# Output and base projections of a transformer block on eight cores: the block loop taken in interleaved pairs

## The chip, the cores and the metric

The kernel runs on the 8 NeuronCores of one Trainium2 chip. All cores run the same program on different rows of the input. The metric is the device time in microseconds (us) of the slowest core; lower is better.

## The reference

```python
x = L0_attn_hidden_states                    # (4, 2048, 2048) float32
xn = _layernorm(x)                           # no scale, no bias
# attention: q, k, v = xn @ Wq.T, xn @ Wk.T, xn @ Wv.T; 16 heads of 128
probs = softmax(q @ k.T * HEAD_DIM ** -0.5)
attn  = (probs @ v) @ Wo.T
# second branch: a base projection and one of 8 rank-16 experts per token
base_out = xn @ W_base.T + b_base
onehot   = one_hot(argmax(softmax(xn @ router_W.T)), 8)
h        = einsum('bsd,erd->bser', xn, A) * onehot[..., None]
delta    = einsum('bser,eor->bso', h, Bw)
return x + attn + base_out + delta * 2.0
```

## The kernel before

Each core owns 1024 tokens of one of the four sequences (QOWN) and computes keys and values for all 2048 tokens of it, so that no core talks to another. Everything is kept transposed: features on the 128 partitions, tokens along the free dimension, matmul operands in bf16, sums in PSUM in float32.

The work has four stages. The first (ln_stats, ln_norm, router, mask_chain) normalizes the tokens and writes xnT, 16 chunks of 128 features by 2048 tokens, which stays on the chip. The second (b2) computes hm, the masked expert activations. The third goes over the 16 heads: the projections of head h are woven into the scores of head h-1, and the result of every head goes into ctall (16 chunks of 128 features by 1024 tokens).

The fourth stage is the one that the change touches. It makes the output in 16 blocks oc of 128 output features by 1024 tokens. A block has two parts:

- gen_dpre(oc), a generator that emits one step at a time. It issues the block's loads: Wo's slice into wot (line 518) and W_base's slice into wbv (line 521) on POOL's queue, both cast from float32 to bf16 on the way, and the residual xT (line 525) on SP's queue. Then it emits 32 matmuls W_base x xnT (line 531: 16 feature chunks, two halves of 512 tokens) and 2 matmuls of the expert weights wbls x hm (line 539), one matmul in each step.
- dpost(oc) emits 32 matmuls Wo x ctall (line 554) onto the same PSUM sums, then one VectorE instruction (line 560) that adds bias and residual and writes outb, and the store outT<-outb on SP's queue (line 565).

Even blocks use PSUM tile psB, weights wqs (Wo) and wks (W_base), and the first half of xst and outb; odd blocks use the upper half of psA, wvs (Wo) and vt (W_base), and the second half. These are the buffers of the attention stage, used again, so every block has two buffers of each kind to alternate with and no third.

Every instruction is recorded by emit() in the order of the Python code, and each engine executes its own instructions in that order. emit() gives an instruction the waits that its buffers need: the last writer of what it reads, the last writer and the readers of what it overwrites. A load of wqs for block oc+2 thus waits for the last matmul of dpost(oc). DMA-issuing instructions stand in the queue of POOL or SP in the order of emission, and one that waits holds all behind it in its queue.

Blocks 0 and 1 are different: gen_dpre(0) and gen_dpre(1) are woven into the scores of the last head, and dpost(0) and dpost(1) follow each other once that head is finished. From block 2 on, gen_dpre(oc) and dpost(oc) alternate.

Of the kernel before, what the change touches and what calls it, by code (L numbers as in the profile page):

```python
# [16 lines left out]
NDC = 16  # L17
# [130 lines left out]
def build_program(debug=False):  # L148
# [28 lines left out]
    with ExitStack() as st:  # L177
# [62 lines left out]
        def xnt(dc, lo, hi):  # L240
            return xnT[:, dc * SEQ + lo: dc * SEQ + hi]
# [262 lines left out]
        def dpsum(oc):  # L504
            if oc % 2 == 0:
                return psB, 0, ["psB0", "psB1"]
            return psA, 1024, ["psA2", "psA3"]

        def gen_dpre(oc):
            ps_t, off, pk = dpsum(oc)  # L510
            if oc % 2 == 0:
                wot, wok_keys = wqs, ["wqs"]
                wbv, wbk_keys = wks[:, 0:D], ["wks"]
            else:
                wot, wok_keys = wvs, ["wvs"]
                wbv, wbk_keys = vt[:, 0:D], ["vt0", "vt1"]
            dstate[oc] = (wot, wok_keys)
            p.emit("pool", lambda E, oc=oc, wot=wot: E.dma_start(
                wot[:, 0:D], wo4[oc].rearrange("p a b -> p (a b)")),
                writes=wok_keys)  # L520
            p.emit("pool", lambda E, oc=oc, wbv=wbv: E.dma_start(
                wbv, wb4[oc].rearrange("p a b -> p (a b)")), writes=wbk_keys)
            sl = oc % 2
            xv = xst[:, sl * D: sl * D + QOWN]
            p.emit("sync", lambda E, oc=oc, xv=xv: E.dma_start(
                xv, xT[oc * 128:(oc + 1) * 128, :]), writes=[f"xs{sl}"])
            yield
            for dc in range(NDC):
                for nb in range(2):
                    p.emit("pe", lambda E, dc=dc, nb=nb, ps_t=ps_t, off=off,  # L530
                           wbv=wbv, wbk_keys=wbk_keys, pk=pk: E.matmul(  # L531
                        ps_t[:, off + nb * 512: off + (nb + 1) * 512],
                        wbv[:, dc * 128:(dc + 1) * 128],
                        xnt(dc, nb * 512, (nb + 1) * 512),
                        start=(dc == 0), stop=False),
                        reads=wbk_keys + XNALL, writes=[pk[nb]])
                    yield
            for nb in range(2):
                p.emit("pe", lambda E, oc=oc, nb=nb, ps_t=ps_t, off=off, pk=pk: E.matmul(
                    ps_t[:, off + nb * 512: off + (nb + 1) * 512],  # L540
                    wbls[:, oc * 128:(oc + 1) * 128],
                    hm[:, nb * 512:(nb + 1) * 512],
                    start=False, stop=False),
                    reads=["wbls", "hm"], writes=[pk[nb]])
                yield

        def dpost(oc):
            ps_t, off, pk = dpsum(oc)
            wot, wok_keys = dstate[oc]
            sl = oc % 2  # L550
            xv = xst[:, sl * D: sl * D + QOWN]
            for dc in range(NDC):
                for nb in range(2):
                    p.emit("pe", lambda E, dc=dc, nb=nb, ps_t=ps_t, off=off, wot=wot: E.matmul(  # L554
                        ps_t[:, off + nb * 512: off + (nb + 1) * 512],
                        wot[:, dc * 128:(dc + 1) * 128],
                        ctall[:, dc * QOWN + nb * 512: dc * QOWN + (nb + 1) * 512],
                        start=False, stop=(dc == NDC - 1)),
                        reads=wok_keys + ["ct"], writes=[pk[nb]])
            p.emit("dve", lambda E, oc=oc, sl=sl, xv=xv, ps_t=ps_t, off=off, pk=pk: E.scalar_tensor_tensor(  # L560
                outb[:, sl * QOWN:(sl + 1) * QOWN],
                ps_t[:, off: off + 1024],
                bbs[:, oc:oc + 1], xv, ALU.add, ALU.add),
                reads=pk + ["bbs", f"xs{sl}"], writes=[f"outb{sl}"])
            p.emit("sync", lambda E, oc=oc, sl=sl: E.dma_start(
                outT[oc * 128:(oc + 1) * 128, :],
                outb[:, sl * QOWN:(sl + 1) * QOWN]),
                reads=[f"outb{sl}"], writes=[], dsem=f"d_out{sl}")
# [28 lines left out]
        attn_av(NH - 1, 1)  # L597
        dpost(0)
        dpost(1)
        for oc in range(2, NDC):  # L600
            for _ in gen_dpre(oc):
                pass
            dpost(oc)

        if debug:
            for name, src, reads in [
# [21 lines left out]
def _get_nc(debug=False):  # L628
    if debug not in _NC_CACHE:
        _NC_CACHE[debug] = build_program(debug)  # L630
    return _NC_CACHE[debug]
# [59 lines left out]
```

How the kernel before makes its waits and increments, by code:

```python
            def body(E, items=items, eng=eng):  # L133
                for it in items:
                    if it[0] == "w":
                        E.wait_ge(sem[it[1]], waitval(it[1], it[2]))
                    else:
                        instr = it[1](E)
                        sname = it[2]
                        if (sname, it[3]) in tgt:
                            instr.then_inc(
                                sem[sname],
                                16 if sname in self.dma_sems else 1)
```

## Time and profile before

| | us |
|---|---|
| median of 2 runs | 1283.63 (1283.35 to 1283.91) |
| the profiled execution, its own time | 1283.7 |
| its span, from the first to the last instruction, slowest core (6) | 1282.2 |
| the spans of the eight cores | 1275.3 to 1282.2 |
| TensorE busy in it | 1142.7 (89%) |

The profile is of one execution on the slowest core. Times inside it count from the start of the span. "PE" is TensorE's matmuls, "PEld" its weight loads, "DVE" VectorE, "SPq" and "POOLq" are the queues on which SP and POOL issue DMAs. PEclk or clock is the share of the full TensorE clock that was granted. L531 means line 531 of the kernel. Tile names leave out buffer numbers, so "psA" is any of psA's banks. Ends of matmuls are modelled: a single one shows 379 ns, though one starts every 216 ns.

### The profile page before, as it was taken

To read this page: it belongs to the slowest core of one execution; us is meant where nothing else is said; L and a number is where in the kernel's file an instruction comes from. 1 tells how busy PE (TensorE), PEld (TensorE's weight loads), DVE (VectorE), ACT (ScalarE), POOL (GpSimd) and SP (SyncE) were. 2 spreads that over 40 slices of the span, in tenths; PEclk is the share of its full clock that TensorE was granted. 3 is DMA by queue.
4 is the path that set the end of the run, shared out by engine and by line. 5 is a ranking of instruction groups with operands and counts; after the bars stand their busy time and mean duration, and the time that the engine had idled before them with its cause. 6 is when DMAs were issued, how large, how long until landed. Compare 5 with 4: busy or idle time off the path is not lost.

```text
span 1282.2 us, 15444 instructions; the slowest of 8 cores (1275.3 to 1282.2 us)
## 1 busy us (share of the span) xinstructions
PE 1142.7 (89%) x5898; PEld 507.1 (40%) x5898; DVE 225.4 (18%) x327; ACT 421.2 (33%) x755; POOL 45.7 (4%) x90
## 2 busy tenths in 40 slices
PE   1348899999999999999999999999999988999998
PEld 1334334333333434333333434333333433444443
DVE  5781111111111111111111111111111100100010
ACT  2451134343343434344343434344343550000000
POOL 1000000000000000000000000000000000000000
PEclk9999999999999999999999999999999998999999
DMA  9841121011110122011111222111111205566654
GB/s 227 250 165 32 18 33 34 18 33 24 27 33 17 34 33 33 17 34 25 25 34 17 33 34 33 17 34 26 25 33 18 49 1 115 132 140 155 165 132 115
DMA packets 19400, 77.62 MB, mean 61 GB/s; under 512 B 2688, under 2 KB 2688, under 8 KB 17280
## 3 DMA queue, kind: packets, MB, share of 16 engines
q0 software_dynamic: 12272, 43.06, 20.3%
q1 hardware_dynamic: 7056, 33.57, 7.4%
q8 instruction: 49, 0.80, 0.3%
q14 instruction: 23, 0.19, 0.1%
HBM read 111.29 MB, written 8.39 MB: 93 GB/s over the span
## 4 chain that ended last, share of the span: by engine, by line
PE 81%; DVE 8%; DMA 4%; ACT 4%; issue 3%; DVEq 0%; ACTq 0%; SPq 0%; POOL 0%; POOLq 0%
PE psB L404 29%; PE psA L404 13%; PE psA L446 9%; PE psC L474 7%; PE psB L531 4%; PE psB L554 4%; PE psA L531 4%; PE psA L554 4%; PE psE L465 2%; DVE st L276 2%; DVE vt L414 2%; DMA xst<-xtok 2%; DVE kt L414 2%; ACT rlb L485 2%; ACT lnl L482 1%
## 5 line engine op out<-in xcount | busy, mean ns | idle before, releaser
L452 ACT ACTIVATE pt<-psA 128x512 bf16<-128x512 f32 x512 | 271.9, 599 | 353.8 <-PE psA L446 353.5
L404 PE MATMUL psB<-xnT,wvs 128*128 128x512 bf16 x768 | 217.5, 379 | 8.7 <-DVE kt L414 8.2
L404 PE MATMUL psA<-xnT,wks 128*128 128x512 bf16 x512 | 193.9, 379 | 8.2 <-DVE kt L414 8.2
L404 PE MATMUL psB<-xnT,wks 128*128 128x512 bf16 x512 | 191.3, 379 | 8.2 <-DVE qt L414 8.2
L446 PE MATMUL psA<-qt,kt 128*128 128x512 bf16 x512 | 143.5, 379 | 3.0 <-ACT vh L437 1.6
L404 PE MATMUL psB<-xnT,wqs 128*128 128x512 bf16 x512 | 119.7, 383 | 1.7 <-ACT maskT L328 1.7
L404 PEld LDWEIGHTS psB<-xnT,wvs 128*128 128x128 bf16 x768 | 74.0, 98 | 106.5 <-issue 21.5
L404 PE MATMUL psA<-xnT,wvs 128*128 128x512 bf16 x256 | 97.0, 379 | 0.0
L474 PE MATMUL psC<-pt,vh 128*128 128x512 bf16 x384 | 88.4, 380 | 0.0
L303 PE MATMUL psA<-idbf,xns 128*128 128x128 bf16 x256 | 29.6, 307 | 63.4 <-DVE xns L295 43.3
L404 PEld LDWEIGHTS psA<-xnT,wks 128*128 128x128 bf16 x512 | 50.0, 98 | 72.3 <-issue 15.6
L404 PEld LDWEIGHTS psB<-xnT,wks 128*128 128x128 bf16 x512 | 50.0, 98 | 72.3 <-issue 15.6
L499 DVE TENSOR_TENSOR ctall<-psC,bc 128x512 bf16<-128x512 f32 x32 | 22.1, 691 | 311.6 <-PE psA L446 257.8
L404 PEld LDWEIGHTS psB<-xnT,wqs 128*128 128x128 bf16 x512 | 50.5, 99 | 63.2 <-issue 4.2
L446 PEld LDWEIGHTS psA<-qt,kt 128*128 128x128 bf16 x512 | 47.4, 98 | 65.4 <-issue 13.7
L531 PE MATMUL psB<-xnT,wks 128*128 128x512 bf16 x256 | 59.3, 388 | 5.1 <-DMA wks<-wb 5.1
L554 PE MATMUL psB<-ctall,wqs 128*128 128x512 bf16 x256 | 58.2, 387 | 1.8 <-DVE ctall L499 1.8
L531 PE MATMUL psA<-xnT,vt 128*128 128x512 bf16 x256 | 57.4, 379 | 0.0
L554 PE MATMUL psA<-ctall,wvs 128*128 128x512 bf16 x256 | 56.6, 379 | 0.0
L474 PEld LDWEIGHTS psC<-pt,vh 128*128 128x128 bf16 x384 | 35.0, 98 | 51.4 <-issue 13.6
L414 DVE CAST vt<-psB 128x512 bf16<-128x512 f32 x48 | 33.2, 692 | 121.3 <-PE psB L404 115.8
L303 PEld LDWEIGHTS psA<-idbf,xns 128*128 128x128 bf16 x256 | 25.9, 142 | 65.0 <-issue 64.9
(75 smaller groups left out, 688.1 us busy)
## 6 DMA issues: line engine op xcount, KB each, us to landing
xst<-xtok SPq DMA_DIRECT2D x8, 1024.0 KB, 9.4
pt<-xtok SPq DMA_DIRECT2D x8, 1024.0 KB, 10.6
wqs<-wq POOLq DMA_DIRECT2D x16, 512.0 KB, 5.1
wks<-wk POOLq DMA_DIRECT2D x16, 512.0 KB, 5.0
wvs<-wv POOLq DMA_DIRECT2D x16, 512.0 KB, 5.0
xst<-xT SPq DMA_DIRECT2D x16, 512.0 KB, 10.2
outT<-outb SPq DMA_DIRECT2D x16, 512.0 KB, 9.6
wqs<-wo POOLq DMA_DIRECT2D x8, 512.0 KB, 6.4
```

The lines of the kernel that those rows point to most:

```text
L276: p.emit("dve", lambda E, xv=xv, i=i, s6=s6: E.bn_stats(s6[:, i * 6:(i + 1) * 6], xv[:, i * 512:(i + 1) * 512]), reads=[xk], writes=[f"st6 ...
L303: p.emit("pe", lambda E, b=b, j=j, dc=dc, xnv=xnv: E.transpose(psabf(b)[:, j * 128:(j + 1) * 128], xnv[:, dc * 128:(dc + 1) * 128], idbf[: ...
L404: col=col, ws=ws: E.matmul(ps_t[:, col:col + 512], ws[:, dc * 128:(dc + 1) * 128], xnt(dc, nb * 512, (nb + 1) * 512), start=(dc == 0), sto ...
L414: dst=dst: E.tensor_copy(dst[:, nb * 512:(nb + 1) * 512], ps_t[:, col:col + 512]),
L446: p.emit("pe", lambda E, kc=kc, qb=qb, bk=bk, ktv=ktv, qtv=qtv: E.matmul(psa(bk), ktv[:, kc * 128:(kc + 1) * 128], qtv[:, qb * 512:(qb + 1 ...
L452: p.emit("act", lambda E, kc=kc, bk=bk: E.activation(pt[:, kc * 512:(kc + 1) * 512], psa(bk), AF.Exp, scale=SCALE), reads=[f"psA{bk}"], wr ...
L465: p.emit("pe", lambda E, kc=kc, j2=j2, r=r: E.matmul(psE[32 * j2:32 * j2 + 1, :], onesc[:], pt[:, kc * 512:(kc + 1) * 512], start=(r == 0) ...
L474: p.emit("pe", lambda E, kc=kc, vhv=vhv: E.matmul(psC[:], vhv[:, kc * 128:(kc + 1) * 128], pt[:, kc * 512:(kc + 1) * 512], start=(kc == 0) ...
L485: p.emit("act", lambda E: E.activation(rlb[:], lnl[:], AF.Exp, scale=-1.0), reads=["lnl"], writes=["rlb"])
L499: p.emit("dve", lambda E, h=h, qb=qb: E.tensor_tensor(ctall[:, h * QOWN + qb * 512: h * QOWN + (qb + 1) * 512], psC[:], bc[:], ALU.mult), ...
L531: wbv=wbv, wbk_keys=wbk_keys, pk=pk: E.matmul(ps_t[:, off + nb * 512: off + (nb + 1) * 512], wbv[:, dc * 128:(dc + 1) * 128], xnt(dc, nb * ...
L554: p.emit("pe", lambda E, dc=dc, nb=nb, ps_t=ps_t, off=off, wot=wot: E.matmul(ps_t[:, off + nb * 512: off + (nb + 1) * 512], wot[:, dc * 12 ...
```

## The change

The loop over the blocks 2 to 15 takes two blocks at a time. It advances the two generators in turn, so their steps alternate: first the loads of both blocks, then one matmul of the even block, one of the odd block, and so on. After that come dpost of the even and dpost of the odd block. Nothing else differs; every instruction is still there, with the same operands.

```diff
         dpost(0)
         dpost(1)
-        for oc in range(2, NDC):
-            for _ in gen_dpre(oc):
-                pass
+        for oc in range(2, NDC, 2):
+            ga, gb = gen_dpre(oc), gen_dpre(oc + 1)
+            while True:
+                a = next(ga, StopIteration)
+                b = next(gb, StopIteration)
+                if a is StopIteration and b is StopIteration:
+                    break
             dpost(oc)
+            dpost(oc + 1)
```

On TensorE, the order before, from dpost(1) to the first half of block 4 (psB is the even blocks' sum, psA the odd blocks'; L531 and L539 are gen_dpre, L554 is dpost):

```order
 L554 MATMUL psA<-ctall,wvs 128x512 x32
 L531 MATMUL psB<-xnT,wks 128x512 x32
 L539 MATMUL psB<-hm,wbls 128x512 x2
 L554 MATMUL psB<-ctall,wqs 128x512 x32
 L531 MATMUL psA<-xnT,vt 128x512 x32
 L539 MATMUL psA<-hm,wbls 128x512 x2
```

The order now on TensorE, at the end of the gen_dpre part of blocks 2 and 3, through their dpost parts, to the first matmuls of blocks 4 and 5:

```order
 L531 MATMUL psB<-xnT,wks 128x512
 L531 MATMUL psA<-xnT,vt 128x512
 L539 MATMUL psB<-hm,wbls 128x512
 L539 MATMUL psA<-hm,wbls 128x512
 L539 MATMUL psB<-hm,wbls 128x512
 L539 MATMUL psA<-hm,wbls 128x512
 L554 MATMUL psB<-ctall,wqs 128x512 x32
 L554 MATMUL psA<-ctall,wvs 128x512 x32
 L531 MATMUL psB<-xnT,wks 128x512
 L531 MATMUL psA<-xnT,vt 128x512
```

Before, 66 matmuls stood between the last read of wvs (L554 on psA) and the first read of vt (L531 on psA); now one stands there. POOL's queue is the same in both programs; here are the loads of blocks 2 to 4, with the semaphores that each waits for:

```order
 L518 DMA wqs<-wo 128x2048 [waits sem_d_wqs,sem_pe]
 L521 DMA wks<-wb 128x2048 [waits sem_d_wks]
 L518 DMA wvs<-wo 128x2048 [waits sem_d_wvs,sem_pe]
 L521 DMA vt<-wb 128x2048 [waits sem_d_vt0]
 L518 DMA wqs<-wo 128x2048 [waits sem_d_wqs,sem_pe]
```

Each load of Wo waits for PE (the dpost part two blocks back), and the load of W_base stands behind it. On SP's queue the order before was, after the stores of blocks 0 and 1:

```order
 L525 DMA xst<-xT 128x1024 [waits sem_d_xs0]
 L565 DMA outT<-outb 128x1024 [waits sem_dve]
 L525 DMA xst<-xT 128x1024 [waits sem_d_xs1]
 L565 DMA outT<-outb 128x1024 [waits sem_dve]
 L525 DMA xst<-xT 128x1024 [waits sem_d_xs0]
```

and it is now:

```order
 L525 DMA xst<-xT 128x1024 [waits sem_d_xs0]
 L525 DMA xst<-xT 128x1024 [waits sem_d_xs1]
 L565 DMA outT<-outb 128x1024 [waits sem_dve] x2
 L525 DMA xst<-xT 128x1024 [waits sem_d_xs0]
 L525 DMA xst<-xT 128x1024 [waits sem_d_xs1]
```

The residuals of a pair now stand together, behind both stores of the pair before.

## Rows read from the trace of the kernel before

**Rows 1.** The page's head and first part; the spans of the cores, core 3.
```profile
span 1282.2 us, 15444 instructions; the slowest of 8 cores (1275.3 to 1282.2 us)
PE 1142.7 (89%) x5898; PEld 507.1 (40%) x5898; DVE 225.4 (18%) x327; ACT 421.2 (33%) x755; POOL 45.7 (4%) x90
...
core 3: 1280.9 us, clock 0.993
```

**Rows 2.** Waits of PE from 1060 us on: total, times, longest.
```profile
PE psB L531 <- DMA wks<-wb: 5.1, 1, 5.1
```

**Rows 3.** Stretch of 30 us: busy of PE, PEld, DVE, ACT, POOL; clock, DMA share, GB/s.
```profile
1090.00:1120.00 30.00, 30.00 (x140) 13.59 (x139) 2.57 (x2) 0.00 (x0) 2.11 (x4) 1.00 0.61 140
```

**Rows 4.** Chain that ended last, in order of time: start us, us, what.
```profile
1041.10 1.29 PE psA L531 x6
...
1065.26 10.70 DMA wks<-wb
...
1076.20 9.04 PE psB L531 x32
...
1092.58 6.91 PE psA L531 x32
1099.48 0.43 PE psA L539 x2
1099.91 6.91 PE psA L554 x32
```

**Rows 5.** Timeline, POOL's issues for one steady block: start, us, what [idle before].
```profile
1107.36 0.53 POOL L518 DMA_DIRECT2D wvs<-wo  x1 [13.19 <-PE psA L554]
1107.88 0.54 POOL L521 DMA_DIRECT2D vt<-wb  x1
```

**Rows 6.** DMA issues from 1092 to 1106 us: KB each, us from issue to landing.
```profile
wqs<-wo POOLq DMA_DIRECT2D x1, 512.0 KB, 6.4
wks<-wb POOLq DMA_DIRECT2D x1, 512.0 KB, 9.8
```

**Rows 7.** Timeline of the dpost parts of blocks 0 and 1 and after.
```profile
1055.44 8.75 PE L554 MATMUL psB<-ctall,wqs 128*128 128x512 bf16 x32 [1.76 <-DVE ctall L499]
...
1064.74 0.53 POOL L518 DMA_DIRECT2D wqs<-wo  x1 [52.32 <-PE psB L554]
...
1071.21 1.28 DVE L560 SCALAR_TENSOR_TENSOR outb<-psA,bbs,xst 128x1024 f32<-128x1024 f32 x1 [5.62 <-PE psA L554]
1071.65 0.53 POOL L518 DMA_DIRECT2D wvs<-wo  x1 [5.85 <-PE psA L554]
1072.17 0.54 POOL L521 DMA_DIRECT2D vt<-wb  x1
1073.01 0.39 SPq L525 DMA_DIRECT2D xst<-xT  x1
```

**Rows 8.** DMA issues from 1064 to 1074 us: KB each, us to landing.
```profile
vt<-wb POOLq DMA_DIRECT2D x1, 512.0 KB, 13.3
xst<-xT SPq DMA_DIRECT2D x1, 512.0 KB, 12.7
```

**Rows 9.** Landing of block 3's vt load on core 3, core 1, core 5.
```profile
DMA to landing us min/median/max: 13.8/13.8/13.8
DMA to landing us min/median/max: 14.0/14.0/14.0
DMA to landing us min/median/max: 12.3/12.3/12.3
```

**Rows 10.** Stretches after the wait, columns as in rows 3.
```profile
1076.00:1080.00 4.00, 3.80 (x10) 1.32 (x11) 0.00 (x0) 0.00 (x0) 0.00 (x0) 0.50 1.04 214
1080.00:1082.00 2.00, 2.00 (x10) 0.93 (x9) 0.00 (x0) 0.00 (x0) 0.00 (x0) 0.95 1.04 166
```

**Rows 11.** DMA queues from 1040 to 1283 us: packets, MB, share of 16 engines.
```profile
q0 software_dynamic: 4032, 14.68, 37.0%
q1 hardware_dynamic: 4320, 15.73, 16.7%
```

## The prediction

> **What bounds the kernel now.** I read the page first: the span is 1282.2 us and TensorE is busy for 89% of it [rows 1]. So only what makes PE wait, or lets it run slower, can move the time much. Second, PE's waits after 1060 us, where the change lies: one wait, 5.1 us, for the load wks<-wb of block 2 [rows 2]. Third, the stretches of 30 us: from 1090 to 1240 PE is busy all the time at the full clock (1.00, the 2.4 GHz level; one of five like rows is shown), while the DMA engines are busy for six tenths [rows 3]. Fourth, the chain in order of time: one matmul follows the other, 32 in 6.91 us, that is 0.216 us each. A block oc is "pre" (32 L531 and 2 L539, 7.34 us) and "post" (32 L554, 6.91 us), 14.25 us together, with no gap [rows 4]. The tail is thus bound by PE alone, and it can be so only because each block's weights land before PE comes to them.
>
> How much room is there? A weight buffer comes free when the block two before has used it, and the load is issued then. In the steady part POOL waits 13.19 us for PE's last matmul of post(oc), then issues wvs<-wo at 1107.36 and, without a further wait, vt<-wb at 1107.88 [rows 5]. The second of such two loads lands 9.8 us after its issue [rows 6]. PE needs it only one whole block (14.25 us) after post(oc) has ended: ready some 10.9 us after that end, it leaves 3.4 us. This is all the slack there is, and it exists because another block's work stands between post(oc) and pre(oc+2).
>
> **The change part by part.** (1) It only reorders PE and SP. The number of matmuls, loads, evictions and stores is the same, POOL's queue is the same row for row. In the pair (oc, oc+1) PE now runs both "pre" parts alternating, then post(oc), then post(oc+1), and at once the alternating "pre" of the next pair, the second matmul of which reads vt.
>
> (2) What has to be in place for that second matmul? vt<-wb stands in POOL's queue behind wvs<-wo of the same block, and this waits for the last matmul of post(oc+1). Call its end T. Before the change a block of 14.25 us lay between T and the first use of vt; now only one matmul of 0.216 us does. PE executes in order, so all that is behind it waits too: the 66 further matmuls of the two "pre" parts, the two "post" parts, both evictions, and through these the stores.
>
> (3) How long? The kernel before shows this very situation once, at its blocks 0 to 3, because post(0) and post(1) already stand back to back there. Post(0) ends, POOL issues wqs and wks at 1064.74; T is 1076.20 - 5.10 = 1071.10; POOL issues wvs at 1071.65 and vt at 1072.17, so T + 1.07 [rows 7]. The engines still have the first two loads in hand, and vt takes 13.3 us to land, where in the steady part the second load of a block takes 9.8 [rows 6, 8]. That is the queue of a pair as the changed kernel has it each time: wqs, wks, a store, and 6.9 us later wvs, vt, a store and an xT load. Between landing (1065.26 + 10.70 = 1075.96) and the first matmul at 1076.20 lie 0.24 us [rows 4, 7]. PE's stall per pair is therefore 1.07 + 13.3 + 0.24 = 14.6 us. For the landing I keep 9.8 us (steady row) and 14.0 (core 1, the longest of the eight in that stretch) as ends, and take 13.3, since its row has the same two bursts with the same distance [rows 9].
>
> (4) The clock. After the 5.1 us of idling the granted clock is 0.50 (1.2 GHz) until 1080, then 0.95 and 1.00 [rows 10]; the 32 matmuls from 1076.20 take 9.04 us instead of 6.91 [rows 4], 2.1 us more. After an idle time of only 1.76 us, the matmuls from 1055.44 took 8.75 us [rows 7], 1.8 more. A stall of 14.6 us will meet the low level as well; I take 2.1 us for each restart (ends 1.8 and, if the lone first matmul or a later rise costs some, 3). The one matmul that runs when wks lands, about T + 5, changes nothing.
>
> (5) Alternating weights and banks. PE loads weights ahead of each matmul already (5898 loads for 5898 matmuls [rows 1]). In the woven part of head 15, two L446 matmuls (other weights, another bank) stand between each six of L531, and the six take 1.29 us [rows 4], the same 0.215. So 0 for 7 x 68 matmuls; a hundredth of a microsecond each either way would be 5 us, and nothing points to it.
>
> (6) Evictions and SP. DVE adds block oc's PSUM in 1.28 us, and for psA this begins at T + 0.1 [rows 7]: done by T + 1.4, hidden behind the load; if the load were not late, it would cost 1.4 us a pair. SP's two xT loads of a pair now stand behind the store of its predecessor's second block, and go out at about T + 2; they are read about 24 us after PE resumes. The first of them lands 12.7 us after its issue at 1073.01 in the row [rows 8], so after vt; the second is behind it on SP's queue. Cost 0, hidden by the "pre" parts. But if its packets compete with vt on the same 16 engines, it could delay vt by its own engine time: SP's queue has 16.7% of 243 us for 30 transfers, 1.35 us each [rows 11]. That is the upper end of this term.
>
> **The sum**, against the profiled execution (span 1282.2 us, 1283.7 with what lies around it; the median of the runs is 1283.63, practically the same). There are seven pairs (2,3) to (14,15). The first has a wait of 5.1 us and a slow restart already: 14.6 - 5.1 = 9.5 us more. The six others: 14.6 + 2.1 = 16.7 us each, 100.2. Together 109.7, and 1283.7 + 109.7 = 1393.4 for core 6. Core 3, at 1280.9 us 1.3 below it, had 13.8 us for vt [rows 1, 9]: 0.5 us more in seven pairs, 3.5 - 1.3 = 2.2 us above core 6, 1395.6. Between the two I forecast 1394.
>
> A weighing of the load's price: the rows have 6.4 us for the first of two steady loads and 13.3 for the delayed one [rows 6, 8]. The Trainium skill ("DMA: Bandwidth & Descriptors", Anatomy of one DMA — SWDGE (gpsimd) path) gives about 2.0 us plus bytes over 436 GB/s for one DMA; as an estimate from that page, two loads of 512 KB behind each other would land after 2.0 + 2 x 1.2 = 4.4 us, PE would stall about 5.2 us, and the kernel would take about 1328 us. The trace disagrees: no load in rows 6 and 8 comes near it, each of them with a store and an xT load beside it.
>
> **The rivals.**
> A. *Steady landing.* The delay of the first pair was a matter of that moment (all cores crossing from attention together), and vt lands after 9.8 us as in the steady part. For it: less DMA work in the longer period. Against: wks took 10.7 us there [rows 4], 9.8 in the steady part, a small difference, and vt's extra comes from the unfinished burst. Stall 1.07 + 9.8 + 0.24 = 11.1; 6.0 + 6 x 13.2 = 85.2; 1369 us.
> B. *Two xT loads in the burst.* Both share the engines with vt and hold it up by 1.35 us: stall 16.0; 10.9 + 6 x 18.1 = 119.5; 1403 us. For it: xT landed only 0.2 us after vt in the first pair, so SP's packets do get their turns; against: the second xT load stands behind the first on one queue. The Trainium skill (same page, Queues, rings and completion order) has the engines take turns among the queues packet by packet, by which B would be a part of the truth.
> C. *A load costs only its own engine time.* POOL's queue: 37.0% of 243 us for 28 loads, 3.2 us each [rows 11]; with 1.2 us to start (9.8 + 0.5 for 9.1 us of work), vt would land 7.6 us after wvs's issue at T + 0.55: stall 8.4; 3.3 + 6 x 10.5 = 66; 1350 us. Against it: every row with company is longer. The page's formula above lies on this side, still further down.
> D. *The other side.* vt is not held behind wvs. Its own last reader, pre(oc+1), ends 13.8 us before T; a load that goes out there and takes 9.8 us is in place at T, and the interleaving is free: 1284 us, or down to 1276.5 if the first pair's 5.1 + 2.1 us went too. It decides where vt's issue falls over 10 us before T. For it: vt's buffer really is free by then. Against: POOL issues in order, and vt follows wvs by 0.5 us in every block of rows 5 and 7.
>
> **How the numbers follow.** Forecast 0.65, A 0.12, B 0.15, C 0.05, D 0.03. The forecast's own range is 1386 (landing 12.3 us, core 5, the shortest [rows 9]) to 1399 (14.0 us and a little more for the restart). For 8 in 10 I reach down to A, 1366, and up past B, 1404. Two per cent, about what a measurement of this kernel can tell from no change, is 26 us: all cases but D are slower. Faster 0.01 and same 0.02 come from D, slower 0.97.
>
> **What would show it.** In the profile after: PE's waits list "DMA vt<-wb" seven times, some 9 to 15 us each (the part after the matmul on wks) and "DMA wks<-wb" seven times with about 5, in sum near 102 us; POOL's second pair of issues 1.1 us or less after each T; granted clock 0.50 in seven restarts, 32 matmuls of which cost 2.1 us more; PE's idle slices in the last 300 us; DMA share of the tail down to about 0.4. Wrong it would be if no wait for vt appears (D), if vt's landings are all below 11 us (A) or above 14.5 (B), or if the interleaved matmuls are not 0.216 us apart at full clock.

## The result, and the profile after

| | before | after |
|---|---|---|
| the profiled execution, its own time | 1283.7 us | 1391.3 us |
| its span, slowest core | 1282.2 us (core 6) | 1389.8 us (core 5) |
| spans of the eight cores | 1275.3 to 1282.2 us | 1369.6 to 1389.8 us |
| ratio | 1 | 1.086 (95% interval 1.084 to 1.088) |

The kernel became 8.6% slower; the forecast was 1394 us. The median of all eleven runs after, 1397.95 us, contains some in which the cores of a die had a lower clock than in the profiled run; the ratio leaves these out.

The page's head and some of its parts, after (compare [rows 1]):

```profile
span 1389.8 us, 15444 instructions; the slowest of 8 cores (1369.6 to 1389.8 us)
PE 1152.9 (83%) x5898; PEld 508.2 (37%) x5898; DVE 225.4 (16%) x327; ACT 421.2 (30%) x755; POOL 45.7 (3%) x90
...
PE   2459999999999999999999999999996855786668
...
L531 PE MATMUL psA<-xnT,vt 128*128 128x512 bf16 x256 | 100.0, 407 | 64.0 <-DMA vt<-wb 64.0
```

The instructions are the same in number. The third line shows PE's busy tenths in 40 equal slices of the span: they are full up to the attention's end and have holes in the last quarter. The interleaved group L531 on psA had no idle time before; now 64.0 us stand before it, all of them ended by the load of vt.

PE's waits from 1050 us on (total, times, longest) answer to [rows 2], where one wait of 5.1 us stood:

```profile
PE psA L531 <- DMA vt<-wb: 64.0, 7, 9.8
PE psB L531 <- DMA wks<-wb: 39.3, 7, 7.0
```

Seven of each, 103.3 us together, so 14.8 us of waiting in each of the seven stalls. Here is one of them in the timeline, for the pair (4,5):

```profile
1107.60 7.07 PE L554 MATMUL psA<-ctall,wvs 128*128 128x512 bf16 x32
...
1108.31 0.53 POOL L518 DMA_DIRECT2D wqs<-wo  x1 [39.72 <-PE psB L554]
1108.83 0.54 POOL L521 DMA_DIRECT2D wks<-wb  x1
...
1115.21 0.53 POOL L518 DMA_DIRECT2D wvs<-wo  x1 [5.85 <-PE psA L554]
1115.73 0.54 POOL L521 DMA_DIRECT2D vt<-wb  x1
1116.57 0.93 SPq L525 DMA_DIRECT2D xst<-xT  x2
...
1120.17 0.58 PE L531 MATMUL psB<-xnT,wks 128*128 128x512 bf16 x1 [5.50 <-DMA wks<-wb]
...
1130.44 0.58 PE L531 MATMUL psA<-xnT,vt 128*128 128x512 bf16 x1 [9.69 <-DMA vt<-wb]
...
1133.22 0.38 PE L531 MATMUL psB<-xnT,wks 128*128 128x512 bf16 x1
...
1139.91 0.38 PE L531 MATMUL psA<-xnT,vt 128*128 128x512 bf16 x1
```

The reader sees the step the forecast rested on: POOL sits 5.85 us before wvs, released by the last L554 on psA, and issues vt right behind it. The dpost part is over at 1114.69; this moment is called T, as in the prediction. PE runs a single matmul when wks is there, and the rest waits till 1130.44, when vt is. That is 15.8 us from T, with one matmul in it. From 1133.22 to 1139.91 there are 32 starts of alternating matmuls, 0.216 us apart, as the matmuls of one block were before [rows 4]. The chain of waits has the same end:

```profile
1107.77 6.92 PE psA L554 x32
...
1115.22 0.52 POOL wvs L518
1115.73 14.47 DMA vt<-wb
1130.20 0.24 issue
1130.44 0.58 PE psA L531
```

The stretches around it (columns as in [rows 3]; they answer to [rows 10]) and the whole tail, first after, then before:

```profile
1120.00:1130.00 10.00, 0.58 (x1) 0.10 (x1) 0.00 (x0) 0.00 (x0) 0.00 (x0) 0.50 1.02 227
1130.00:1132.00 2.00, 1.56 (x4) 0.58 (x5) 0.00 (x0) 0.00 (x0) 0.00 (x0) 0.50 0.10 41
1134.00:1138.00 4.00, 4.00 (x21) 1.79 (x19) 0.00 (x0) 0.00 (x0) 0.00 (x0) 1.00 0.00 0
...
1060.00:1380.00 320.00, 216.68 (x933) 93.49 (x932) 19.26 (x15) 0.00 (x0) 14.75 (x28) 0.84 0.42 92
```

```profile
1060.00:1283.00 223.00, 212.66 (x976) 95.61 (x974) 20.55 (x16) 0.00 (x0) 14.77 (x28) 0.98 0.59 137
```

PE comes back at the low level, 0.50, and is at full clock some 3 us later here (its matmuls show 0.38 us again from 1133.22 on). Over the tail the clock is 0.84 and the DMA engines' share 0.42, against 0.98 and 0.59 before.

### The profile page after: what moved, and what is told of

Same layout as the page of the kernel before. It is cut to its first block, busy times and chain, and to the rows that moved or that the text cites. A ratio compares the mean times of both kernels' runs of the same rounds, so it can differ in the third digit from the quotient of the medians.

```text
span 1389.8 us, 15444 instructions; the slowest of 8 cores (1369.6 to 1389.8 us)
## 1 busy us (share of the span) xinstructions
PE 1152.9 (83%) x5898; PEld 508.2 (37%) x5898; DVE 225.4 (16%) x327; ACT 421.2 (30%) x755; POOL 45.7 (3%) x90
## 4 chain that ended last, share of the span: by engine, by line
PE 76%; DMA 10%; DVE 7%; ACT 3%; issue 3%; POOL 0%; DVEq 0%; ACTq 0%; SPq 0%; POOLq 0%
PE psB L404 27%; PE psA L404 12%; PE psA L446 8%; DMA vt<-wb 7%; PE psC L474 6%; PE psA L531 5%; PE psB L531 4%; PE psB L554 4%; PE psA L554 4%; PE psE L465 2%; DVE st L276 2%; DVE vt L414 2%; DVE kt L414 2%; DMA xst<-xtok 2%; ACT rlb L485 1%
## 5 line engine op out<-in xcount | busy, mean ns | idle before, releaser
L404 PE MATMUL psB<-xnT,wks 128*128 128x512 bf16 x512 | 191.3, 379 | 8.2 <-DVE qt L414 8.2
L531 PE MATMUL psA<-xnT,vt 128*128 128x512 bf16 x256 | 100.0, 407 | 64.0 <-DMA vt<-wb 64.0
L531 PE MATMUL psB<-xnT,wks 128*128 128x512 bf16 x256 | 101.2, 412 | 39.3 <-DMA wks<-wb 39.3
L404 PEld LDWEIGHTS psB<-xnT,wks 128*128 128x128 bf16 x512 | 50.0, 98 | 72.4 <-issue 15.6
L404 PEld LDWEIGHTS psA<-xnT,wks 128*128 128x128 bf16 x512 | 49.9, 98 | 72.3 <-issue 15.6
L531 PEld LDWEIGHTS psA<-xnT,vt 128*128 128x128 bf16 x256 | 26.5, 104 | 101.4 <-issue 75.6
L554 PE MATMUL psB<-ctall,wqs 128*128 128x512 bf16 x256 | 56.6, 379 | 1.8 <-DVE ctall L499 1.8
L554 PE MATMUL psA<-ctall,wvs 128*128 128x512 bf16 x256 | 56.6, 379 | 0.0
L531 PEld LDWEIGHTS psB<-xnT,wks 128*128 128x128 bf16 x256 | 26.4, 103 | 75.4 <-issue 50.3
L560 DVE SCALAR_TENSOR_TENSOR outb<-psB,bbs,xst 128x1024 f32<-128x1024 f32 x8 | 10.3, 1284 | 268.4 <-PE psB L554 268.4
## 6 DMA issues: line engine op xcount, KB each, us to landing
xst<-xT SPq DMA_DIRECT2D x16, 512.0 KB, 13.6
```

The source lines that it names most:

```text
L404: col=col, ws=ws: E.matmul(ps_t[:, col:col + 512], ws[:, dc * 128:(dc + 1) * 128], xnt(dc, nb * 512, (nb + 1) * 512), start=(dc == 0), sto ...
L531: wbv=wbv, wbk_keys=wbk_keys, pk=pk: E.matmul(ps_t[:, off + nb * 512: off + (nb + 1) * 512], wbv[:, dc * 128:(dc + 1) * 128], xnt(dc, nb * ...
```

## The experiments

**W_base's loads ahead of Wo's, matmuls still interleaved.** Only POOL's queue is changed, the rest is the changed kernel.

```diff
-            p.emit("pool", ... wot <- wo4[oc] ...)
+            if oc < 2:
+                p.emit("pool", ... wot <- wo4[oc] ...)
             p.emit("pool", ... wbv <- wb4[oc] ...)
             p.emit("sync", ... xv <- xT ...)
             yield
+            if oc >= 2:
+                p.emit("pool", ... wot <- wo4[oc] ...)
+                yield
```

> The changed kernel with POOL's order of loads altered from block 2 on: both loads of W_base (wks, vt) of a pair stand ahead of both loads of Wo (wqs, wvs). The interleaving of the matmuls stays. My theory (the time went into vt's load, held behind wvs's wait for the last dpost matmul): wks and vt go out when the gen_dpre part of the pair before has ended, 13.8 us before T, and are in place at T; no wait for a DMA is left, and no slow restart, also at the first pair. What remains is the eviction of psA (1.28 us from T + 0.1), for which the second matmul waits some 1.5 us, 7 times 1.5 = 10.5 us. Expected 1284.9 - 7.2 + 10.5, about 1288 us (1284 to 1292). The rival that alternating weights and PSUM banks costs by itself expects that most of the 110 us stays: over 1370 us.

Measured: 1286.6 us median, ratio 1.002 (1.001 to 1.003). PE's waits in the tail:

```profile
PE psA L537 <- DVE outb L566: 9.2, 7, 1.3
PE psB L560 <- DVE ctall L499: 1.8, 1, 1.8
PE psE L494 <- ACT rlb L485: 0.6, 1, 0.6
```

No wait for a DMA is left, and 110 us have come down to 3, while the matmuls still alternate. What remains is the eviction of psA, 1.3 us in each of seven pairs, which the long stall had covered. The 3 us are not the whole price of the interleaving, since this order of the queue makes the kernel before faster too (next run, 1275.6 us beside it). Against that one the interleaved kernel is 11 us slower, of which the evictions explain 9.2; under 2 us are left for the alternation of 476 matmuls. So the alternation costs next to nothing. What costs is that PE's order leaves no time between the event that releases the queue (the last matmul of dpost) and the first use of what stands behind it in the queue.

**The same order of loads in the kernel before.**

> The kernel before (no interleaving) with the load of W_base ahead of the load of Wo in POOL's queue from block 2 on. My theory: wks of block 2 no longer stands behind wqs's wait for dpost(0), so the one wait of 5.1 us and the slow restart behind it (2.1 us) go, and nothing else changes: 7.2 us less, ratio 0.994, about 1277.5 us (1276 to 1280). The rival that this wait is set by the DMA engines' load at that moment, and not by the place in the queue, expects no difference, ratio 0.999 to 1.001.

Measured: 1275.6 us, ratio 0.994 (0.992 to 0.995); a second time, on another chip, 1276.1 us and 0.994 (0.993 to 0.996). That is some 8 us less, 1 us more than expected. The wait on wks is gone from PE's list, and the loads land sooner, as they no longer go out two at a time. The DMA issues from 1060 us on (KB each, median us to landing):

```profile
vt<-wb POOLq DMA_DIRECT2D x7, 512.0 KB, 5.3
wvs<-wo POOLq DMA_DIRECT2D x7, 512.0 KB, 6.8
wks<-wb POOLq DMA_DIRECT2D x6, 512.0 KB, 5.4
```

Wks and vt, each issued some 7 us away from the loads of Wo, land 5.4 and 5.3 us after their issue here, where the second of two together took 9.8 [rows 6].

**Gen_dpre parts in a row, not woven.** Loads and stores stand as in the changed kernel.

```diff
-            while True:
-                a = next(ga, StopIteration)
-                b = next(gb, StopIteration)
-                if a is StopIteration and b is StopIteration:
-                    break
+            next(ga)
+            next(gb)
+            for g in (ga, gb):
+                for _ in g:
+                    pass
```

> The changed kernel with its loads issued as there (both blocks' loads first, then dpost, dpost), but the gen_dpre matmuls of the two blocks one block after the other and not alternating. My theory: at T PE waits only for wks (issued 5.9 us before T, landing after 9 to 11 us: some 5 us of wait) and restarts slowly (2.1 us), and vt has 7.3 to 9.4 us more: it lands about when PE comes to it, 0 to 1 us of wait. At the first pair almost nothing is added; the six others 7.2 to 8 us each: 43 to 50 us, 1284.9 + 46, about 1330 us (1322 to 1338). A rival by which only the alternation of weights and banks costs expects 1285 us; one by which the back-to-back dpost parts alone decide, wherever vt is first read, expects 1394 us.

Measured: 1334.9 us median, ratio 1.039 (1.036 to 1.043). PE's waits on the profiled core 0, then on core 5, and three lines of the list of cores:

```profile
PE psB L531 <- DMA wks<-wb: 24.8, 7, 5.1
PE psA L531 <- DMA vt<-wb: 3.5, 4, 1.4
```

```profile
PE psB L531 <- DMA wks<-wb: 37.2, 7, 6.1
PE psA L531 <- DMA vt<-wb: 4.3, 5, 1.1
```

```profile
core 0: 1333.4 us, clock 0.970
...
core 3: 1310.9 us, clock 0.995
...
core 5: 1329.8 us, clock 0.981
```

The sum of waits is 28.3 us on core 0 and 41.5 us on core 5 instead of 103.3: with 7.3 us of other matmuls between, vt is late by about 1 us where it is late at all on these two, and by 5.1 us at most on any core (core 4). So the seven or more microseconds of cover decide, as the theory has it. Core 5 fits the theory in its parts too, with 5.3 us of wait for wks and 0.6 for vt in the mean of the pairs.

That the slowest core also came near 1330 us is partly chance. Core 0 waited 13 us less than core 5 and still ended later, for a reason that no theory here contains: between 1080 and 1240 us the clock granted to it was 0.81 wherever it was not 0.50 (core 1 had the same, cores 2 and 3 did not). Its 32 matmuls of a dpost took 8.57 us instead of 6.91 there, which also gave the loads more time. A dpost of core 0 and one stretch of it:

```profile
1089.67 8.57 PE L554 MATMUL psB<-ctall,wqs 128*128 128x512 bf16 x32
```

```profile
1160.00:1180.00 20.00, 19.75 (x75) 8.10 (x76) 0.66 (x1) 0.00 (x0) 0.22 (x1) 0.81 0.09 35
```

Core 3 was faster than the theory. It waited 7 us less than core 5, and besides not every wait was followed by the low level. These two waits are nearly equal, and the 32 matmuls behind the first cost 1.7 us more than those behind the second:

```profile
1135.70 8.75 PE L531 MATMUL psB<-xnT,wks 128*128 128x512 bf16 x32 [3.67 <-DMA wks<-wb]
...
1169.75 7.07 PE L531 MATMUL psB<-xnT,wks 128*128 128x512 bf16 x32 [3.72 <-DMA wks<-wb]
```

**The stall filled with matmuls.** 64 extra ones before each pair, the result unused.

```diff
         for oc in range(2, NDC, 2):
+            for _ in range(64):
+                p.emit("pe", ... matmul psE <- idbf, xnT[0:512] ...)
             ga, gb = gen_dpre(oc), gen_dpre(oc + 1)
```

> The changed kernel with 64 extra matmuls of 512 columns (idbf by xnT into psE, result unused) between dpost(oc+1) and the next pair: 13.8 us of PE work in each of the seven stalls. My theory has each stall followed by a restart at the low clock that costs 2.1 to 2.5 us. With the filling the clock stays at 1.00 and PE waits only some 0.5 to 1 us for vt, so the time falls by about 7 times 2.3 = 16 us against the changed kernel, less up to 5 us where vt lands earlier than 13.8 us: 1380 us (1376 to 1388). A rival by which the stall alone costs and the restart is free expects no fall: 1394 to 1400 us.

Measured: 1380.8 us, ratio 1.075 (1.074 to 1.077), 13 us below the changed kernel though PE does 97 us more work. PE's wait for vt, and the tail's stretch:

```profile
PE psA L531 <- DMA vt<-wb: 7.4, 5, 2.5
```

```profile
1060.00:1370.00 310.00, 302.57 (x1392) 136.07 (x1391) 18.94 (x15) 0.00 (x0) 14.76 (x28) 0.99 0.43 95
```

The stall's length did not move (64 x 0.216 x 7 = 97 us of filling and 7.4 us of waiting, 104 in all, against 103.3): it is set by the load, not by what PE does meanwhile. The clock went from 0.84 to 0.99 and gave back 13 us, near the 16 expected. Not all of the slow restarts went. In this pair PE waited only 2.3 us, began at full clock, and then ran eight matmuls at the low level all the same (0.63 us where 0.38 is usual, 0.43 us apart):

```profile
1129.44 0.38 PE L531 MATMUL psA<-xnT,vt 128*128 128x512 bf16 x1 [2.29 <-DMA vt<-wb]
...
1130.50 0.63 PE L531 MATMUL psA<-xnT,vt 128*128 128x512 bf16 x1
...
1133.72 0.38 PE L531 MATMUL psA<-xnT,vt 128*128 128x512 bf16 x1
```

**What sets vt's landing: xT loads and stores taken away.** Three kernels, all the changed one with transfers left out: both xT loads of a pair, only the odd block's (second) one, and both with the stores of blocks 0 to 13. The diff is that of the last; the first has only its upper half, and the second has there the condition oc < 2 or oc % 2 == 0.

```diff
+            if oc < 2:
+                p.emit("sync", ... xv <- xT ...)
-            p.emit("sync", ... xv <- xT ...)
...
+            if oc >= 14:
+                p.emit("sync", ... outT <- outb ...)
-            p.emit("sync", ... outT <- outb ...)
```

> The changed kernel without the xT loads of blocks 2 to 15 (14 loads; the residual of these blocks is left out, the old contents of the buffers are added in its place). They go out right behind vt's load, two in a burst, on the other queue. My theory: they hardly hold vt up, since vt's own queue and the burst before it set its landing, and they stand behind a store on theirs: the time stays within 5 us of the changed kernel's (1389 to 1396 us). Rival B of the prediction, by which the two loads share the engines and the memory with vt (1.35 us of engine time each): vt lands 1.3 to 2.7 us earlier, 7 times that, 9 to 19 us less: 1375 to 1386 us.

> The changed kernel without the xT loads of blocks 2 to 15 and without the stores of blocks 0 to 13 (the residual and these blocks' output are left out). Only the four weight loads of a pair are on the DMA engines. My theory: a weight load costs some 3.2 us of engine time, wqs and wks are done before T + 0.5, and wvs and vt land 7.6 us after wvs's issue: vt takes 7 to 8 us from its issue, the stall is 8.4 us, and the kernel takes 1350 us (1340 to 1360). If instead the other core on the same memory and not this core's own stores and loads sets the landing, vt still takes 10 us or more: over 1365 us.

> The changed kernel itself, beside the two without transfers on the same chip: 1391 to 1398 us, ratio 1.084 to 1.088; vt's landing some 12 to 14 us, about 100 us of waits for vt and wks in seven stalls.

> The changed kernel without the xT loads of the odd blocks from 3 on (the second of the two in each burst, the one that the change moved in; those blocks' residual is left out and the buffer's old contents added). Leaving out both made the kernel 12 us faster, where I had expected under 5. Theory 1: the second load, behind the first on its queue, is as harmful as the first, since both still move while vt does: half of the 12 us goes, ratio 1.080 to 1.083. Theory 2: vt has landed before the second gets its turn, and only the first matters: ratio as the changed kernel's, 1.084 to 1.088. Theory 3: the second does it all: 1.075 to 1.078.

| left out | median us | ratio (95%) |
|---|---|---|
| nothing (the changed kernel, once more) | 1393.9 | 1.086 (1.083 to 1.090) |
| second xT load | 1391.5 | 1.085 (1.083 to 1.086) |
| both xT loads | 1380.9 | 1.077 (1.075 to 1.079) |
| both, and the stores | 1362.0 | 1.062 (1.059 to 1.064) |

The second row was taken on another chip than the rest, so the ratios compare, not the times. The issues of vt in the tail of each, in the table's order (the slowest core; median us to landing):

```profile
vt<-wb POOLq DMA_DIRECT2D x7, 512.0 KB, 12.8
```

```profile
vt<-wb POOLq DMA_DIRECT2D x7, 512.0 KB, 13.7
```

```profile
vt<-wb POOLq DMA_DIRECT2D x7, 512.0 KB, 11.7
```

```profile
vt<-wb POOLq DMA_DIRECT2D x7, 512.0 KB, 8.4
```

I was wrong to expect nothing from the xT loads: without both, the kernel is 0.9% faster, in rival B's range. The mean over all cores fell by 10 us, and the cores came closer together. Without the second xT load alone nothing changes beyond the interval. So the one that the change moved into the burst costs nothing that can be seen, and my row of before, with its single xT load, was a fair stand-in. That it is the first of them that counts is concluded from these two runs; leaving out the first alone was not tried. The Trainium skill ("DMA: Bandwidth & Descriptors", Queues, rings and completion order) lets the engines take turns between the queues packet by packet; the runs agree for what moves beside vt (a store and one xT load). The second xT load stands behind these on its queue: on core 5 of the changed kernel the first landed 0.2 to 0.5 us after vt in the seven bursts, the second 1.2 to 1.8 us after it. With neither stores nor xT loads vt still takes 8.4 us, and the kernel 1362 us where I expected 1350: even alone, two weight loads behind each other are slower than their engine time of 3.2 us each by [rows 11] made me think. By how much the other cores' loads slow them was not tried.

**A version that beats both.** W_base's loads first, and gen_dpre(2) used to fill the two waits in the last head's attn_av; then each gen_dpre one block ahead.

```diff
-            if oc % 2 == 0:
-                return psB, 0, ["psB0", "psB1"]
-            return psA, 1024, ["psA2", "psA3"]
+            if oc % 3 == 0:
+                return psB, 0, ["psB0", "psB1"]
+            if oc % 3 == 1:
+                return psA, 1024, ["psA2", "psA3"]
+            return psA, 0, ["psA0", "psA1"]
...
-        attn_av(NH - 1, 1)
+        for oc in (2, 3):
+            for _ in gen_dpre(oc, early=True):
+                pass
+        attn_av(NH - 1, 1, fill=gen_dpre(2))
         dpost(0)
         dpost(1)
-        for oc in range(2, NDC):
+        dlate(2)
+        for oc in range(3, NDC):
             for _ in gen_dpre(oc):
                 pass
-            dpost(oc)
+            dpost(oc - 1)
+        dpost(NDC - 1)
```

With early=True a block emits only its W_base load; dlate(2) emits Wo's load and xT of block 2. Of the filling, 12 steps (11 matmuls, since the first step emits none) stand before the broadcast matmul (line 494 of the kernel before) and the rest behind it.

> A version meant to beat both: the kernel before with W_base's loads ahead of Wo's, as in the run on that, and the gen_dpre matmuls of block 2 moved into the two waits of the last attn_av (before and after the matmul that broadcasts the reciprocal sums), on the PSUM banks psA0 and psA1 that the scores have left; from there on each gen_dpre stands one block ahead of its dpost, with three PSUM places in turn. In the run before, PE still waits 1.8 us for ctall and 0.6 us for rlb there and comes back at the low clock (1.8 us more). With the filling these go: about 4 us less than that version's 1276.5, so 1272 to 1274 us, ratio 0.990 to 0.992. If the matmuls in the gap only push the exp, copy and multiply back, it is as that version, 0.993 to 0.995.

> The kernel before with W_base's load ahead of Wo's, once more, beside the version above on the same chip: 1276 to 1277.5 us, ratio 0.993 to 0.995.

Measured: 1272.5 us, ratio 0.992 (0.990 to 0.993), 3.6 us below the version without the filling, run beside it. PE around the last attn_av:

```profile
1052.05 2.54 PE L548 MATMUL psA<-xnT,wks 128*128 128x512 bf16 x11
1054.52 0.38 PE L497 MATMUL psE<-rlb,onesr 1*128 1x512 bf16 x1
1054.84 4.71 PE L548 MATMUL psA<-xnT,wks 128*128 128x512 bf16 x21
1059.38 0.59 PE L556 MATMUL psA<-hm,wbls 128*128 128x512 bf16 x2
1059.81 5.56 PE L580 MATMUL psB<-ctall,wqs 128*128 128x512 bf16 x25
```

No gap is left between them (one wait of 1.0 us for wks, of block 4, is new: its load stands behind wvs's again and took 13.9 us to land), and the L580 matmuls start at full clock (25 in 5.56 us), where the same matmuls of before took 8.75 us for 32 [rows 7].

## Why the prediction was right

The profiled execution took 1391 us, the ratio times the 1284.9 us of before beside it gives 1395, and the forecast was 1394. The forecast's mechanism, not a rival's, is what the trace shows; that the number came so close is partly luck (step 3 and the sum for the cores, below). Point by point:

- *Step 2, vt held behind wvs.* Shown by the timeline above and by the run with W_base's loads first, in which the cost went with the place in the queue. Rival D needed POOL to issue vt early; with the queue changed so that it does, 1286.6 us is measured. That is within 1 us of rival D's lower figure, 1276.5 (the first pair's wait is gone as well), with 9.2 us of eviction waits on top.
- *Step 3, 14.6 us per stall.* Measured 14.8 us of waiting on the profiled core (103.3 / 7), 15.3 us from T to the restart with the slow matmul on wks in between. But the stand-in row fitted better than it had to: vt's median landing was 13.6 us there, and on core 7 only 10.1 us, where the kernel's span was 1369.6 us, rival A's number. The metric takes the slowest of eight cores, and that one has landings as in the first pair of before. A repeated run had 12.8 us on its slowest core. I took 13.3 for all pairs; right for the slowest core, too long for a typical one (the medians of the other seven are 10.1 to 14.0 us, five of them below 12.2).
- *Step 4, 2.1 us per restart.* From T of the first pair (1067.01) to the end of the last matmul (1385.40) are 318.4 us; seven pairs of 28.5 us and 103.3 us of waits leave 15.6, or 2.2 each, with some 0.4 us for the matmul on wks that runs at the low level in the middle of the stall. The filled stall gave 13 us of it back.
- *Step 5, alternation 0.* Right within 2 us: 1286.6 against 1275.6 us with the same order in POOL's queue, 9.2 of the 11 us being eviction waits, and matmuls 0.216 us apart in the trace.
- *Step 6, 1.4 us for the eviction if the load were not late.* Measured 1.3 us as soon as the load was early. *The moved xT load 0, at most 1.35 us.* Right for the moved one; the first xT load, already in my row, is worth about 12 us in the seven stalls by the runs without xT loads.
- *The sum for core 3 and core 6* (1395.6 and 1393.4) was too high for both: their spans were 1388.9 and 1380.3 us, so 5 and 12 us less once the 1.5 us around the span are added. Core 5, the fastest of before (1275.3), was last instead, 114.5 us longer. The forecast of the slowest core fell right because the misses offset each other. Which core is slowest changes from run to run after the change, since the stalls differ between cores by several microseconds.

| lines | expected | measured, core 5 |
|---|---|---|
| waits for vt and wks | 7 and 7, near 102 us | 7 and 7, 103.3 us |
| DMA share of the tail | about 0.4 | 0.42 |
| restarts | 0.50, 2.1 us each | 0.50, 2.2 us each |

Open remain why two cores were granted 0.81 in the run without weaving, why like waits there sometimes led to the low level and sometimes not, and what the neighbour cores add to a landing.

## What to carry to other kernels

When work is reordered, look at each load's release event and its first use and count the work between the two; this kernel had 14 us there and needed 11, and batching two blocks took it away while every instruction stayed the same. In an in-order queue put first the load whose buffer comes free first: here a load that waited held up the one behind it, whose buffer had been free for 13.8 us, and swapping the two took the ratio from 1.086 to 1.002. A stand-in for a pattern that the change makes common can often be found once in the trace of before, at a start or an end of a loop; here it gave the price of queueing (13.3 us), which the steady part's 9.8 us did not.

## What was not expected of the hardware

- The low level of the clock is not tied to the length of one wait. It came after waits of 1.76 us [rows 7] and, with a delay of three matmuls, of 2.3 us (the rows of the filled stall); it came after one wait of 3.67 us and not after another of 3.72 us (core 3 of the run without weaving); and seven waits of 1.3 us for the eviction left the clock at 1.00. After each of the seven long stalls on the profiled core of the changed kernel it was 0.50.
- Loads of one size, 512 KB (bf16 on the chip), took 5.4 us to land when issued by themselves, 6.4 and 9.8 us as first and second of two with a store and an xT load, and 13 to 14 us behind an unfinished burst on the slowest cores: what else was under way changed the landing by more than a factor of two.
- Doing 97 us more of matmuls made the kernel 13 us faster than the changed one, because it kept the clock up while PE would have waited anyway. It stayed 7.5% slower than the kernel before.
